# Moving the latent attention's scores, maxima and subtractions to an earlier place in each pipeline step

## The reference

```python
h = layernorm(x) * (1 + ca) + sa
Q, K, V = h @ wq, h @ wk, h @ wv                      # 16 heads of 8
local = softmax(window(Q @ K.T))                      # each block of 32 rows sees itself and the block before
GQ = h @ wgq                                          # 8 latent heads of 8
GK, GV = mean8(h @ wgk), mean8(h @ wgv)               # 64 latents: means over 8 rows
lsc = GQ @ GK.T / sqrt(8), masked causally
rem = softmax(lsc) @ GV @ r_out                       # the latent ("remote") branch
out = (sigmoid(..) * (local @ V) + sigmoid(..) * rem) @ w_out
x = x + ga * out                                      # then the second norm
h2 = layernorm(x) * (1 + cb) + sb
x = x + gb * ffn(h2, weights mixed per batch entry by a gate)
```

## Time and profile before

| | |
|---|---|
| median of 3 runs | 748.62 us (748.38 to 749.38) |
| time of the profiled execution | 748.97 us |
| span from its first to its last instruction | 747.2 us |
| granted TensorE clock, mean | 0.979 of full speed |
| busy: PE, PEld, DVE, ACT, POOL | 86%, 68%, 72%, 52%, 39% of the span |

### The profile page before, as it was taken

How to read it: one execution, slowest core, us unless ns; L and a number is a source line. 1 busy time by engine, 2 the same in 40 slices (tenths; PEclk the granted TensorE clock), 3 DMA queues, 4 the chain that set the end, 5 groups by cost and what they waited for, 6 DMA issues and landing times.

```text
span 747.2 us, 24120 instructions
## 1 busy us (share of the span) xinstructions
PE 645.6 (86%) x8822; PEld 506.4 (68%) x8822; DVE 538.1 (72%) x1241; ACT 384.9 (52%) x910; POOL 294.9 (39%) x415
## 2 busy tenths in 40 slices
PE   5588888788888878888887888888779999999998
PEld 3366666566666656666665666666558999898996
DVE  5568788888878888887888888788755546273552
ACT  2256655666665566666555666655543223423233
POOL 2256555455555545555554555555530000000000
PEclk9699999999999999999999999999978999999999
DMA  3757111000101100010110001010140010100101
GB/s 99 174 78 96 32 24 32 21 21 21 28 22 24 31 21 21 21 28 21 24 32 21 21 21 28 21 24 18 29 44 0 10 35 15 32 24 21 34 9 49
DMA packets 65797, 24.84 MB, mean 33 GB/s; under 512 B 38440, under 2 KB 64360, under 8 KB 65648
## 3 DMA queue, kind: packets, MB, share of 16 engines
q1 hardware_dynamic: 64320, 18.25, 10.2%
q0 software_dynamic: 1456, 6.31, 5.6%
HBM read 16.13 MB, written 8.40 MB: 33 GB/s over the span
## 4 chain that ended last, share of the span: by engine, by line
PE 42%; DVE 26%; ACT 15%; issue 14%; POOL 1%; ACTq 1%; DVEq 1%; DMA 0%; SPq 0%; POOLq 0%
DVE mx L561 10%; PE SB L820 7%; PE WB L808 7%; DVE rden L634 5%; ACT PT L443 5%; PE SB L927 5%; PE WB L795 4%; PE SB L795 4%; ACT xn_d L449 4%; DVE Pr L568 3%; ACT Pr L403 3%; PE SB L882 2%; PE SB L931 2%; ACT PL L435 2%; PE WB L970 2%
## 5 line engine op out<-in xcount | busy, mean ns | idle before, releaser
L336 POOL TENSOR_TENSOR KM<-K_ch,bd_scale 128x1024 f32<-128x1024 f32 x32 | 60.6, 1893 | 125.2 <-ACT K_ch L411 125.2
L634 DVE RECIPROCAL rden<-SB 128x256 f32<-128x256 f32 x32 | 56.2, 1758 | 54.5 <-PE SB L931 54.5
L506 ACT ACTIVATE Pr<-WB,mb1T 128x256 f32<-128x256 f32 x128 | 49.8, 477 | 75.7 <-PE WB L808 75.6
L561 DVE TENSOR_REDUCE mx<-SB 128x8 f32<-128x512 f32 x128 | 87.2, 681 | 1.5 <-PE SB L882 1.5
L403 ACT ACTIVATE Pr<-Pr 128x512 f32<-128x512 f32 x128 | 80.8, 631 | 10.8 <-DVE Pr L568 7.2
L568 DVE TENSOR_TENSOR Pr<-SB,mx 128x512 f32<-128x512 f32 x128 | 84.6, 681 | 0.0
L358 POOL TENSOR_TENSOR PT_sum<-PT 128x512 f32<-128x512 f32 x64 | 80.3, 1275 | 3.8 <-ACT PT L443 3.8
L443 ACT COPY PT<-SB 128x512 f32<-128x512 f32 x128 | 66.1, 622 | 0.0
L896 PE MATMUL SB<-ident,Pr 128*128 128x128 f32 x512 | 63.0, 276 | 0.9 <-ACT Pr L403 0.9
L820 PE MATMUL SB<-Pr,GA 128*128 128x256 f32 x256 | 61.2, 381 | 0.0
L835 PE MATMUL WB<-hT,wk 128*128 128x256 f32 x64 | 23.3, 448 | 43.2 <-DVE PlB L582 43.2
(11 more groups left out here) (195 smaller groups left out, 1518.5 us busy)
## 6 DMA issues: line engine op xcount, KB each, us to landing
x_all<-in_L_attn_x SPq DMA_DIRECT2D x32, 128.0 KB, 2.1
v_rows<-V_rows SPq DMA_DIRECT2D x32, 128.0 KB, 1.8
VBD<-v_rows SPq DMA_DIRECT2D x128, 32.0 KB, 1.8
TW<-in_L_ffn_TW POOLq DMA_DIRECT2D x16, 256.0 KB, 9.5
GA<-ga_rows POOLq DMA_DIRECT2D x1, 2048.0 KB, 10.5
out_x<-attT SPq DMA_DIRECT2D x16, 128.0 KB, 1.8
out_x<-y_ga SPq DMA_DIRECT2D x16, 128.0 KB, 1.8
PT<-in_L_ffn_W SPq DMA_DIRECT2D x2, 256.0 KB
```

Of the source, the lines that this page charges most:

```text
L336: nc.gpsimd.tensor_tensor(KM[:, :, W:KW], bc(K_ch[:], [P, 4, S], 1), bc(bd_scale[:], [P, 4, S], 2), ALU.mult).then_inc(km_ready, 1)
L561: nc.vector.tensor_reduce(mx[:, k, :], SB[k][:].rearrange("p (h j) -> p h j", h=8), AX.X, ALU.max).then_inc(mx_ready, 1)
L634: nc.vector.reciprocal(rden[:], SB[2][:, S:2 * S]).then_inc(rden_ready, 1)
```

## The change

In each step, PE does `latent_scores` behind the product with `w_out` and ahead of the second norm's transposes and the values, where it stood behind the first norm's transposes. The latent branch's output product (`rem_n`, `r_out`) moves from behind the values to behind the first norm's transposes. On DVE the latent maxima and subtractions move ahead of the inversion of the local sums; they stood between `rem_g` and the local maxima and among these. On POOL `GKBD` moves from behind `PT_sum` to directly behind `KM`. No instruction is added or removed, and no shape changes.

```diff
@@ POOL, step
                     nc.gpsimd.tensor_tensor(KM[:, :, W:KW], bc(K_ch[:], [P, 4, S], 1), bc(bd_scale[:], [P, 4, S], 2), ALU.mult
                                             ).then_inc(km_ready, 1)
+                    pool.wait_ge(gq_ready, 2 * (b + 1))
+                    nc.gpsimd.tensor_tensor(GKBD[0:NL], bc(GKT[:], [NL, LH, NL], 1),
+                                            bc(head[0:NL, 0:LH], [NL, LH, NL], 2), ALU.mult).then_inc(gkbd_ready, 1)
...
-                if has(it, 1):
-
-                    b = it - 1
-                    pool.wait_ge(gq_ready, 2 * (b + 1))
-                    nc.gpsimd.tensor_tensor(GKBD[0:NL], bc(GKT[:], [NL, LH, NL], 1),
-                                            bc(head[0:NL, 0:LH], [NL, LH, NL], 2), ALU.mult).then_inc(gkbd_ready, 1)
@@ DVE, step
                 if has(it, 3) and not tail:
                     output_times_ga(it - 3)
+                if has(it, 1):
+                    b = it - 1
+                    for t, pl, m in latent_tiles:
+                        latent_maximum(b, t, m)
+                    for tile in latent_tiles:
+                        latent_lowered(b, *tile)
...
-                    for t, pl, m in latent_tiles:
-                        latent_maximum(b, t, m)
-                    latent_lowered(b, *latent_tiles[0])
                     maximum(b, 0)
-                    latent_lowered(b, *latent_tiles[1])
@@ PE, step
                     last.then_inc(y_done, 1)
+                if has(it, 1):
+                    latent_scores(it)
                 if has(it, 4):
...
                 if has(it, 2):
                     values(it)
-                    pe.wait_ge(remn_ready, it - 2 + 1)
-                    bank_free(pe, it, (3, yga_ready, 1, 1), (1, vrows_ready, 1, 1))
-                    for t in range(T):
-                        last = mm(WB[3][:, t * P:(t + 1) * P], r_out[:, t, :], rem_n[:], start=True, stop=True)
-                    last.then_inc(rem_done, 1)
...
-                if has(it, 1):
-                    latent_scores(it)
+                if has(it, 2):
+                    pe.wait_ge(remn_ready, it - 2 + 1)
+                    bank_free(pe, it, (3, yga_ready, 1, 1), (1, vrows_ready, 1, 1))
+                    for t in range(T):
+                        last = mm(WB[3][:, t * P:(t + 1) * P], r_out[:, t, :], rem_n[:], start=True, stop=True)
+                    last.then_inc(rem_done, 1)
+                if has(it, 1):
                     scores(it)
```

## The result

The changed kernel takes 773.13 us (median of 4 runs, 772.33 to 775.51), the kernel before 748.9 (4 runs): a ratio of 1.033, 95% interval 1.031 to 1.035. The change costs 24 us; 772 was forecast. The profiled execution of the changed kernel took 772.47 us, its span is 770.7 us against 747.2, at a granted clock of 0.982.

A forecast was written before the change was run, and what follows sets the result against it. It took a chain passing from engine to engine, with no engine full, to bound the 16.34 us step. 28 x 0.70 + 0.82 + 0.84 + 1.7 + 0.4 = 23.4 us more gave a median of 772, range 763 to 782.

The forecast's parts named there:

- The step's bound, and PE's queue holding the sums: Loop step of 16.34 us: a chain across engines sets it; PE's own queue, not POOL, holds the sums before DVE's inversion.
- The hole ends where the products may begin: PE's 0.88 us wait ahead of the second norm's transposes ends at 304.43; the latent products must await `GVBD`, ending at 304.41.
- The slip: Delay of DVE's inversion from latent products ahead of PE's transposes and values: about 1.42 us, bounds 1.2 to 1.6.
- From `a_loc` to the maximum: From the end of `a_loc` through PE's local scores to DVE's first local maximum: 2.11 us, read in step 32.
- The sum for a step: One loop step: first local maximum 1.30 us later, second 0.70 us later, since `PlB` no longer stands between them.
- the point of turning: The change pays only if the inversion's delay s is under 0.72 us; a step changes by s - 0.12 - 0.60 us.
- DVE's cover ahead of the inversion: DVE's latent maxima and subtractions end at about 307.6, the sums at 307.9: hidden with 0.3 us to spare.
- The edits costed at nothing: Moves of `rem_n`'s product on PE and `GKBD` on POOL: no cost, though `PT_sum` ends some 0.2 us later.
- The steps outside the loop: Added time: step 1 about 0.4 us, step 2 about 1.7, step 3 0.84, step 32 0.82.
- The hole takes the products: Rival: latent products run in PE's 0.88 us wait, delay 0.58 us, some -4 us, 744.5; with a 736 variant, 6 in 100.
- A dearer slip: Rival: PE's order costs over 1.6 us, or DVE's latent work outlasts the sums: 780 to 790, 7 in 100.
- The clock falls: Rival: PE's granted clock falls for the products in each step, +1.31 us each, 37 us more, 809; 3 in 100.

## Why the prediction was right

- **The step's bound, and PE's queue holding the sums.** Right. Everything given to PE ahead of the values reached the inversion; with DVE's order of before the step grew by 1.39 us.
- **The hole ends where the products may begin.** Right, and the experiment that takes this wait away, and changes no order, turns 1.033 into 0.979. The wait for the readers of `WB[1]` and `WB[0]`, `GVBD` last, is therefore what made the change a loss.
- **The slip.** Forecast 1.42 to 1.43 us, measured 1.44. The products' term, forecast at 1.39 us from their start to the transposes, was 1.36. They start 0.15 us behind the end of `GVBD` (300.57 against 300.42) where 0.06 was forecast, and the values follow the transposes after 0.32 us where it was 0.36 before.
- **From `a_loc` to the maximum.** 2.11 us from step 32 of before, 2.10 in the loop of the changed kernel.
- **The sum for a step.** +0.70 forecast, +0.73 measured. It also names the point of turning, s = 0.72 us, which was tested at s = 0.20 and s = 1.44.
- **DVE's cover ahead of the inversion.** Right, with 0.19 us to spare where I had 0.3: `PlB` ends at 303.75 and the inversion starts at 303.94.
- **The edits costed at nothing.** POOL's move and `rem_n`'s product: no measurable change in either. POOL's move is needed all the same: without it the changed kernel takes 880 us.
- **The steps outside the loop.** Step 1 cost 0.75 us in place of 0.4, step 2 1.16 in place of 1.7; steps 3 and 32 together 0.97 + 0.76 = 1.73 in place of 1.66. The sum of 24.06 us at step 32 becomes 23.5 in the span. The difference is gone by the inversion of step 33 (552.22 and 575.54, 23.32 later). In the kernel before, the granted clock is 0.50 over that step's latent values, in the changed kernel 1.00 (rows in the last section), and PE comes to the product with `w_out` behind them at 549.09 and 572.00, only 22.91 later. That the span comes within 0.1 us of the forecast 23.4 is in part luck: the loop cost 0.8 us more than forecast, steps 1 and 2 together 0.2 less, and what the clock gave back wasn't forecast.
- **The rivals.** "The hole takes the products" named the right condition; it holds when the banks are changed, not in this kernel. Its price of -4 us was too small, since I took extents for the work (a slip of 0.58 us where 0.20 was measured): it gave -14 to -15. The starts that tell the difference were in the trace of before. "A dearer slip" didn't come, with 1.44 us inside the bounds of 1.2 to 1.6. "The clock falls" didn't occur in this kernel, with a granted clock of 1.00 over its step. Nor did PE's busy share go to 82%: over the step from 303.94 it is 14.43 of 17.07 us, 85% as before, since the rows of the same work are longer in sum than the 13.95 us of before. The Trainium skill's page "TensorE: Matmul & The Clock Gate", section "A second HAM failure mode: psum-queue depth-cycling", reports a bf16 kernel in which short pauses between groups of matmuls in each iteration make the clock swing between its two levels. Pauses of 1.0 and 1.24 us in each step of 17 us did not do so here.

## What to carry to other kernels

Work moved into the idle time of one engine (DVE) has to be fed by another (PE), and if that one's queue holds the very work the idle engine is waiting for, the hole is filled and the end of the hole moves too. Before such a move, look for the last wait of the feeding instructions: here for PSUM banks that other readers still held, and two free banks turned 3% of loss into 2% of gain. And when work is taken away from behind a wait, ask what the engine will meet next; the local scores had been 0.12 us from being the bound, which one step in which nothing covered them (step 32) showed to 0.01 us.

## What the runs showed of the hardware that I had not expected

- With a pause of PE of 3.00 us in each step the granted clock is 0.51 for the products behind it, and 1.00 in the window of the values and sums. The four products took twice as long (2.70 us in place of 1.36). At 1.34 us in each of 31 steps that is, by an estimate, 41 of the 106 us by which that kernel is slower than the changed one. Pauses of 1.0 and 1.24 us in each step of the loop left the clock at 1.00.
- A fall followed shorter pauses too, outside the loop. At the start of its part of step 33 PE pauses for 2.00 us in the kernel before and, a little further on, for 1.79 us in the changed one, and soon after the clock is at half. One row of each timeline, the pause in brackets, and the windows of that step's latent values, of before and then of the changed kernel:

```profile
541.74 0.44 PE L904 MATMUL WB<-ident,PlA 128*128 128x128 f32 x2 [2.00 <-ACT PlB L470]
...
567.00 0.96 PE L895 MATMUL SB<-ident,Pr 128*128 128x128 f32 x4 [1.79 <-ACT Pr L400]
...
547.30:549.30 2.00, 2.00 (x25) 1.44 (x26) 0.09 (x1) 2.00 (x5) 1.66 (x3) 0.50 0.89 92
...
570.80:572.50 1.70, 1.70 (x31) 1.33 (x29) 0.39 (x1) 1.70 (x5) 1.28 (x3) 1.00 0.99 96
```

  In the changed kernel the clock is 0.55 from 568.80 to 570.80 us and 1.00 again for the latent values; in the kernel before it is still 0.50 there.
- On DVE a 512-column subtraction that needs the maximum directly ahead of it starts 0.72 us behind that one's start; one that needs an older result follows at 0.60 to 0.61. With 256 columns it is 0.45 us in place of 0.33. In the changed kernel `PlA` stands between the large maximum and `PlB`, and neither pays the 0.1 us.
